# Decoder layer on one core: cross-attention steps regrouped in cycles of two, with a third probability buffer

## The reference, cut to what matters

```
q = x Wq^T + bq;  k = ctx Wk^T + bk;  v = ctx Wv^T + bv      # ctx: 1500 x 256 per sequence
scores = clip(q k^T / 4, -50, 50), masked places -50
probs = softmax(scores);  out = (probs v) Wo^T + bo, scaled, layer norm, added to x
```

## Time and profile before

| | |
|---|---|
| median of 3 runs | 1390.54 us (1390.42 to 1393.0) |
| the profiled execution, own time | 1393.26 us |
| its span | 1391.5 us |
| TensorE matmul busy | 1369.0 us, 98% |
| TensorE weight load busy | 1171.2 us, 84% |
| VectorE busy | 997.8 us, 72% |
| ScalarE busy | 720.7 us, 52% |
| GpSimd busy | 518.4 us, 37% |
| mean granted TensorE clock | 0.998 of full speed |

### The profile page before, as it was taken

How to read it: one execution, slowest core, us unless ns; L and a number is a source line. 1 busy time by engine, 2 the same in 40 slices (tenths; PEclk the granted TensorE clock), 3 DMA queues, 4 the chain that set the end, 5 groups by cost and what they waited for, 6 DMA issues and landing times.

```text
span 1391.5 us, 55868 instructions
## 1 busy us (share of the span) xinstructions
PE 1369.0 (98%) x25409; PEld 1171.2 (84%) x25409; DVE 997.8 (72%) x1821; ACT 720.7 (52%) x943; POOL 518.4 (37%) x494
## 2 busy tenths in 40 slices
PE   8999999999999999999999999999999999999997
PEld 6788888886888888888888888888888888888884
DVE  5788788785356867777676867677776868677766
ACT  3555454543555555555555555555554555555550
POOL 4656666651324233333323332433333242333310
PEclk9999999999999999999999999999999999999999
DMA  7010001010411211121202121121212122111100
GB/s 193 1 36 2 31 1 32 2 52 1 129 52 48 64 48 50 47 65 33 70 31 78 51 62 50 47 64 33 65 32 80 33 64 65 48 51 47 51 3 8
DMA packets 38957, 66.81 MB, mean 48 GB/s; under 512 B 3749, under 2 KB 36962, under 8 KB 38722
## 3 DMA queue, kind: packets, MB, share of 16 engines
q1 hardware_dynamic: 38722, 63.24, 15.4%
HBM read 61.40 MB, written 1.84 MB: 45 GB/s over the span
## 4 chain that ended last, share of the span: by engine, by line
PE 72%; DVE 2%; issue 0%; POOL 0%; DVEq 0%
PE proj_ps L1460 20%; PE proj_ps L1451 20%; PE score_ps L1478 15%; PE sum_ps L1503 13%; PE side_ps L1538 2%; PE side_ps L1552 1%; PE side_ps L1520 1%; PE side_ps L1545 1%; DVE amax L1338 0%; DVE hidden L1360 0%; DVE sig L1370 0%; DVE hidden L1371 0%; PE side_ps L1527 0%; DVE exps L1260 0%; DVE totals L1282 0%
## 5 line engine op out<-in xcount | busy, mean ns | idle before, releaser
L1212 ACT ACTIVATE exps<-score_ps 125x1792 f32<-125x1792 f32 x192 | 320.8, 1671 | 430.7 <-PE score_ps L1478 430.7
L1260 DVE TENSOR_SCALAR exps<-exps,top 125x896 f32<-125x896 f32 x384 | 289.0, 795 | 21.8 <-ACT exps L1212 17.5
L1478 PE MATMUL score_ps<-spread,keys 32*125 32x112 f32 x6144 | 219.0, 279 | 0.0
L1251 DVE COPY vals<-proj_ps 125x512 f32<-125x512 f32 x192 | 129.5, 688 | 115.6 <-PE proj_ps L1460 113.3
L1503 PEld LDWEIGHTS sum_ps<-exps,vals 125*32 125x32 f32 x12288 | 163.0, 110 | 47.1 <-issue 34.2
L1478 PEld LDWEIGHTS score_ps<-spread,keys 32*125 32x125 f32 x6144 | 184.8, 183 | 15.4 <-issue 0.3
L1503 PE MATMUL sum_ps<-exps,vals 125*32 125x56 f32 x12288 | 191.5, 215 | 0.0
L1140 POOL TENSOR_TENSOR low<-raw_early,high 128x500 fp32r<-128x500 f32 x64 | 84.4, 1323 | 217.8 <-PE proj_ps L1451 217.1
L1140 POOL TENSOR_TENSOR low_early<-raw_early,high_early 128x500 fp32r<-128x500 f32 x62 | 90.3, 1475 | 167.7 <-PE proj_ps L1451 167.7
L1204 ACT ACTIVATE keys<-proj_ps,b_k 128x500 f32<-128x500 f32 x192 | 130.0, 677 | 23.6 <-PE proj_ps L1451 19.8
L326 POOL TENSOR_TENSOR swapped<-swapped,sin 128x448 f32<-128x448 f32 (+1 forms) x72 | 85.6, 1192 | 79.4 <-ACT swapped L597 78.5
(11 more groups left out here) (186 smaller groups left out, 2742.7 us busy)
## 6 DMA issues: line engine op xcount, KB each, us to landing
raw_early<-in_ctxT SPq DMA_DIRECT2D x64, 500.0 KB, 4.1
raw<-in_ctxT SPq DMA_DIRECT2D x32, 500.0 KB, 3.5
w_q<-in_attn_Wq SPq DMA_DIRECT2D x4, 512.0 KB, 8.5
out<-y_out SPq DMA_DIRECT2D x16, 112.0 KB, 2.3
rows<-in_x SPq DMA_DIRECT2D x1, 1344.0 KB, 17.8
raw_early<-in_attn_Wo SPq DMA_DIRECT2D x1, 1024.0 KB, 18.0
raw_early<-in_ffn_gate_wT SPq DMA_DIRECT2D x1, 1024.0 KB, 5.3
raw_early<-in_ffn_val_wT SPq DMA_DIRECT2D x1, 1024.0 KB, 4.9
```

The lines of the kernel that those rows point to most:

```text
L1212: nc.scalar.activation(exps[t % 2][:, :, :, :].rearrange("p h r n -> p r h n"), score_ps[0:TILE, :, 0:2 * QW].rearrange("p r (h n) -> p r ...
L1251: nc.vector.tensor_copy(vals[r][:, 2 * q:2 * q + 2, :, 0:HD], proj_ps[q][0:TILE, :].rearrange("p (k h d) -> p k h d", k=2, d=HD))\
L1260: nc.vector.tensor_scalar(tile, tile, LIMIT_LO, top[:, n, at:at + 1], ALU.max, ALU.min)\
L1478: ins = nc.tensor.matmul(score_ps[0:TILE, r, to:to + HE * S], keys[c % 2][32 * r:32 * r + 32, k, (at + half) * TILE:(at + half + 1) * TILE ...
```

## The change

The number of probability buffers goes from two to three. The loops of TensorE, ScalarE and VectorE go over chunks (m) with an even step e = 2m and an odd step o = 2m + 1. On TensorE a cycle is S(e), A(e - 2), A(e - 1), S(o), tail step e, P01, tail step o, P23. The exponential of step t now waits for the value products of step t - 3. ScalarE does both exponentials first, then the key copies and splits. VectorE does limits of e, tail step e, limits of o, tail step o, value copies; the tail steps 0 and 10 stand ahead of the limits of e. GpSimd and the DMA queue are not changed. All instructions are the same in number and shape. The three loops `body` in the diff are ScalarE's, VectorE's and TensorE's, in this order.

```
-GATES = (7, 8)
-AFTER = (2, 5)
+TWINS = NT // 2
+SLOTS = 3
...
-        exps = [sb(f"exps{n}", [TILE, 2, HR, QW]) for n in range(2)]
+        exps = [sb(f"exps{n}", [TILE, 2, HR, QW]) for n in range(SLOTS)]
...
                 act.wait_ge(scores_ready, NT * i + t + 1)
                 if warm:
-                    act.wait_ge(probs_used, NT * i + t - 1)
+                    act.wait_ge(probs_used, NT * i + t - SLOTS + 1)
...
             def body(i, first, last):
+                for m in range(TWINS):
+                    x = PC * i + m
+                    exp_twin(i, 2 * m, not first or 2 * m >= SLOTS)
+                    if not first and m == 4:
+                        gate_tanh(i - 1, 1)
+                    exp_twin(i, 2 * m + 1, not first or 2 * m + 1 >= SLOTS)
+                    for p in range(DC):
+                        if not (last and m == PC - 1):
+                            keys_out(x + 1, p, (m + 1) % 2)
+                        if not (last and m >= PC - 2):
+                            split_high((m + 2) % 3, 2 * i + (m + 2) // 3 + 1, m % 2, p)
+                    if not first and m == 3:
+                        gate_tanh(i - 1, 0)
...
+            AHEAD = (0, 10)
             def body(i, first, last):
+                for m in range(TWINS):
+                    e, o = 2 * m, 2 * m + 1
+                    if e in AHEAD and e in tail:
+                        tail[e]()
                     for k in range(2):
+                        limit(i, e, k)
+                    if e == 0 and not first:
                         read_sums(i - 1, 1)
+                    if e == BN:
                         read_sums(i, 0)
+                    if e in tail and e not in AHEAD:
+                        tail[e]()
+                    for k in range(2):
+                        limit(i, o, k)
+                    if o in tail:
+                        tail[o]()
...
+                    for q in range(2) if not (last and m == PC - 1) else ():
+                        values_copy(PC * i + m + 1, q, (m + 1) % 2)
...
             def body(i, first, last):
-                for t in range(NT):
-                    c, half = divmod(t, 2)
-                    scores(i, t, not first or t >= 1)
-                    if t in tail and t not in AFTER:
-                        tail[t]()
-                    if not (last and c == PC - 1):
-                        for p in (2 * half, 2 * half + 1):
-                            piece(PC * i + c + 1, p, (c + 1) % 2)
-                    if t in tail and t in AFTER:
-                        tail[t]()
...
-                    if t:
-                        add_up(i, t - 1, not first or t - 1 >= BN)
-                    elif not first:
-                        add_up(i - 1, NT - 1, True)
+                for m in range(TWINS):
+                    e, o = 2 * m, 2 * m + 1
+                    x, r = PC * i + m + 1, (m + 1) % 2
+                    scores(i, e, not first or e >= 1)
+                    for n in (e - 2, e - 1):
+                        if n >= 0:
+                            add_up(i, n, not first or n >= BN)
+                        elif not first:
+                            add_up(i - 1, NT + n, True)
...
+                    scores(i, o, True)
+                    if e in tail:
+                        tail[e]()
+                    if not (first and m == 0) and not (last and m == PC - 1):
+                        piece(x, 0, r)
+                        piece(x, 1, r)
+                    if o in tail:
+                        tail[o]()
+                    if not (last and m == PC - 1):
+                        piece(x, 2, r)
+                        piece(x, 3, r)
```

More of the change, by code:

```diff
@@ L1257, in limit @@
                 dve.wait_ge(exps_ready, NT * i + t + 1)
-                tile = exps[t % 2][:, half, :, :].rearrange("p r n -> p (r n)")
+                tile = exps[t % SLOTS][:, half, :, :].rearrange("p r n -> p (r n)")
                 n, at = 2 * i + t // BN, 2 * (t % BN) + half
@@ L1398, in body @@
                 tail = {} if first else tail_steps(i - 1, False)
[L1399 to L1400 removed]
+                for m in range(TWINS):
+                    e, o = 2 * m, 2 * m + 1
+                    if e in AHEAD and e in tail:
+                        tail[e]()
                     for k in range(2):
[L1402 to L1406 removed]
+                        limit(i, e, k)
+                    if e == 0 and not first:
                         read_sums(i - 1, 1)
[L1408 removed]
+                    if e == BN:
                         read_sums(i, 0)
[L1410 to L1419 removed]
+                    if e in tail and e not in AHEAD:
[4 more added lines that the diff above has]
+                        tail[o]()
+                    if last and o == BN + 3:
+                        divide(i, 0)
+                    for q in range(2) if not (last and m == PC - 1) else ():
+                        values_copy(PC * i + m + 1, q, (m + 1) % 2)
                 if not first:
@@ L1429, in _ @@
             body(LAST, False, True)
-            for half in range(2):
-                limit(LAST, NT - 1, half)
             read_sums(LAST, 1)
@@ L1564, in body @@
                 tail = {} if first else tail_steps(i - 1)
-                for t in range(NT):
-                    c, half = divmod(t, 2)
-                    scores(i, t, not first or t >= 1)
-                    if t in tail and t not in AFTER:
-                        tail[t]()
-                    if not (last and c == PC - 1):
-                        for p in (2 * half, 2 * half + 1):
-                            piece(PC * i + c + 1, p, (c + 1) % 2)
-                    if t in tail and t in AFTER:
-                        tail[t]()
-                    if last and c == PC - 1:
+                for m in range(TWINS):
[7 more added lines that the diff above has]
+                            add_up(i - 1, NT + n, True)
+                    if first and m == 0:
+                        piece(x, 0, r)
[4 more added lines that the diff above has]
+                    if not (first and m == 0) and not (last and m == PC - 1):
+                        piece(x, 0, r)
+                        piece(x, 1, r)
+                    if o in tail:
[3 more added lines that the diff above has]
+                        piece(x, 3, r)
+                    else:
                         pe.wait_ge(vals_ready, 2 * PC * PAIRS)
                         spare(3)
-                    if t == NT - 1 and not first:
+                        add_up(i, e, True)
+                    if o == NT - 1 and not first:
                         tail[NT]()
-                    if t:
-                        add_up(i, t - 1, not first or t - 1 >= BN)
-                    elif not first:
-                        add_up(i - 1, NT - 1, True)
             for p in range(4):
```

13 lines of the change are left out of this document (2 added, 11 removed).

## The result

The changed kernel takes **1450.07 us** (median of 4 runs, 1447.12 to 1453.38), the kernel before 1391.7 beside it on the same chip: a ratio of **1.0422**, 95% interval 1.0407 to 1.0436. Forecast were 1377.3 us, range 1371 to 1387. It is slower by 58, not faster by 13.

The account below looks back on a forecast made before the run. TensorE, busy 98% of the span, was taken to bound the kernel. 94 cycles x 0.18 give -16.9 us, tail steps +3.7, together -13.2: 1390.54 - 13.2 = 1377.3 us, range 1371 to 1387.

Parts of the forecast that it names:

- a pair of sequences: TensorE's six cycles of a pair: 0.18 us saved in each, 0.25 a pair added for tail steps.
- entering and leaving a mode: On TensorE, each stage S, A or P pays on entering and on leaving, 0.08 to 0.13 us on leaving.
- the new wait for the exponential: On TensorE, S(o) waits until exp(e) has read its scores: 0.13 us in every cycle.
- the tail steps: Odd tail steps 5, 7, 9, 11 between P01 and P23 save nothing there: 0.25 us a pair, +3.7 us.
- the late release: Rival: TensorE starts S(o) 0.15 us after the exponential, not 0.05; 9.4 us lost, 1386.7 us; chance 0.12.
- the late tail: Rival: in m = 1 the tail runs late, TensorE waits for `xq` at `turn_rows`; 1396.8 us; chance with a loss 0.05.
- the full saving: Rival: two mode changes a cycle saved on TensorE without the new wait; -33 + 3.7, 1361.2 us; chance 0.04.
- The change, part by part: Prediction's section pricing TensorE's new cycle by trace rows: 9.75 us, 0.18 less than 9.93; then tail steps, other engines, ends.
- some other semaphore: Rival: late value copies or keys keep the old spacing at P01 or P23; 1394.2 us; chance 0.04.
- Ends ... Nothing, within 0.5: First and last chunk: A(8) and A(9) move, the rest stays in line; no cost, within 0.5 us.
- six changes of mode: TensorE's mode changes in one chunk before the change, about 1.06 us together; four now, two fewer being 0.35 a cycle.
- both of its spreads: Uncertainty of the passage from P to S, 7.5 us, and of the tail term, 0.15 to 0.40 a pair.

Follow-up runs that it names:

- e1: The half-products run: changed kernel with the second half of every step's value products left out, output incomplete; 1381.78 us.
- e14: e9 with 40 fillers for 48 in first cycles, 46 for 42 in the fourth and fifth, and a start 24 instructions earlier; 1385.54 us (0.9954).
- e3: Changed kernel with TensorE filled by met waits, in three lots, to 512 instructions a cycle, block borders in the middle of the dense run; 1423.28 us (1.0226).
- e4: e3 with 128 more fillers in its first cycle, so that one block is just the two A; 1667.93 us.
- e2: Changed kernel with 64 already met wait instructions put once ahead of the first cycle; 1458.6 us.
- e9: Changed kernel with met waits as fillers, at most 48 a cycle, 2 or 3 behind each term of the sum in all four pieces; 1387.8 us (0.9979).
- e11: e9 with seven twelfths of a cycle's fillers in P01, five in P23, and a start 24 instructions earlier; 1407.81 us (1.0127).
- e12: Kernel before, order untouched, with the fillers of e11 at the same places in the pieces; 1409.59 us (1.0133).
- e13: Kernel before, order untouched, with exactly the fillers of e9; 1417.19 us (1.0183).
- e5: e3 with each filler an increment of an unused semaphore in place of a met wait, same number and places; 1557.72 us (1.1191).

## Why the prediction was wrong, point by point

**What held.** The terms of the sum that were worked out from rows came out, wherever no block border fell into the run:

| | forecast | changed kernel, undisturbed cycles |
|---|---|---|
| S(e) to S(o) | 2.93 | 2.92 to 2.93 |
| release by exp | 0.05 | 0.04 to 0.05 |
| plain cycle | 9.75 | 9.75 to 9.76 |
| cycle with `project` (m = 1) | 10.61 | 10.61 |
| a pair of sequences | 63.26 - 6 x 0.18 + 0.25 = 62.43 | none undisturbed; 62.47 to 62.49 in e1, 62.47 to 62.50 in seven pairs of e14 |

So entering and leaving a mode, the new wait for the exponential and the tail steps (0.29 a pair for the 0.25 taken) are right to some hundredths. Of the rivals the late release fell with the 0.04, the late tail with the undisturbed m = 2 (9.92; the one wait for `xq`, 1.2 us, is behind the last pair), and the full saving with the exponential's end, which does bind. The half-products run, 1381.8, lies within the range and 4.5 above its point; the first cycle's 2.8 us are most of that.

**What failed.** The step is the first of "The change, part by part": it prices S, A, A, S as the sum of their rows. Each row holds while TensorE has its instructions. 384 of them in 4 us is a density that occurs nowhere in the kernel before (5.15 us at the least), and I did not ask who delivers them: the delivery stands in the sum at nothing, without a reason. The rivals were all waits for a result, or for another engine; "some other semaphore" came nearest and is not it. The sum lacked some 50 us of holes and some 20 us of half clock behind them. The case that it is this, and not another consequence of the order, rests on e3 against e4: the same work, the same fillers behind the first cycle, another phase, 1423 against 1668; on e1 and e2; on the packets, which end 1.2 to 1.5 us ahead of the end of each hole; and on e9 and e14, which keep all of the change and its work and are faster than before.

The Trainium skill ("Runtime: NRT & Kernel Launch", Instruction fetch mechanics) says that an engine's instructions come in blocks of 16 KiB, 256 of them, through a FIFO, and that crossing a border is mostly hidden. The first half agrees with the queue's 16 KB packets and with the distances between the holes. The second held in the kernel before and does not hold here: the holes were 0.5 to 3.1 us from one matmul's start to the next.

**Smaller misses.** "Ends ... Nothing, within 0.5" was wrong by 3.0 us in the changed kernel and 2.8 in e1: the first cycle keeps TensorE's order but not ScalarE's, and piece 2 waits for keys. I had looked at TensorE's order of that cycle alone. Two sums of the prediction are off without effect: its six changes of mode (0.19 + 0.19 + 2 x 0.15 + 2 x 0.20) make 1.08 and not 1.06, and with both of its spreads, 7.5 us and 0.15 to 0.40 a pair, the forecast's own range is 1368 to 1387 and not 1370 to 1385.

**Left open.** What asks for a packet: against the entry into the block ahead its start varies by 3 us. What the 1.2 to 1.5 us between a packet's end and its use are. Whether P01 inside the burst, with VectorE's order fitted to it, would do without fillers wasn't tried; nor was a first cycle with the key copies ahead of exp(o). Why e9's fillers cost the old order 25 us, and the new one only some 6 (1387.8 against 1381.8 in the half-products run), is settled in part: their phase was worked out for the new order, and in the old one some 5 us are late blocks; the rest is not accounted for. With the fillers of e11 and e12 it was the other way, 26 us in the new order (1407.8 against 1381.8) and 18.6 in the old one.

## What to carry to other kernels

Before work with many short instructions is put together on one engine, count its instructions against time: here TensorE got 256 more within 2.5 to 5.0 us, mostly some 3.6, and a run of 384 in 4 us, in 94 cycles, cost some 70 us where the reordering was to save 13. A pause that is released by nothing, in the middle of a stage, moving when an instruction is added far ahead, is the sign. Work of few long instructions between the short ones (the pieces here) gives the next block time to come, so its place can be worth more than the changes of mode. Fillers are a tool to find the cause rather than a cure: the best of these runs with fillers gained 0.5%.

## What the runs showed of the hardware

- TensorE's stream arrives in packets of 16 KB, one per 256 instructions, 0.9 to 1.7 us long. At the 33 holes of the changed kernel a block was used 1.2 to 1.5 us after its packet's end and 2.5 to 5.0 us after the block ahead of it was begun; in e13, with fillers in the old order, at late blocks up to 5.5 us.
- A hole of that kind can be followed by several us at half clock: 44.9 us in the changed kernel, 204.8 us with a hole in each cycle (e4), 6.8 before. With the holes gone it was 6.8 (e9) and 13.7 us (e14).
- A met wait as a filler takes the sequencer 0.106 us. 16 to 18 in one lot show as 0.3 to 0.7 us of idle TensorE (e3); 2 or 3 behind each term of a sum are nearly hidden (e9). An increment of a semaphore takes 0.151 us, with pauses up to 1.4 us (e5).
